# Graph layers: nine groups counted late and not stored, 22 groups multiplied in layer 0, seven sets of features in ten as parts

## The chip, the core and the metric

The kernel runs on one core of a Trainium2 chip. The metric is the device time of one execution in microseconds (us); lower is better. The core has five engines with a queue of instructions each: PE (TensorE, matmuls; PEld are its weight loads), DVE (VectorE), ACT (ScalarE), POOL (GpSimd) and SP (SyncE, which here only issues DMAs). They wait for each other through semaphores.

## The reference

Two graph layers over 6250 nodes and 100000 edges, edges sorted by target, width 128, float32:

```python
def _layer(h, edge_feats, src, dst, deg, iso, Wn, Ws, Wi, num_nodes):
    msg = (h[src] + edge_feats) @ Wn.T
    agg = segment_sum(msg, dst, num_nodes) / maximum(deg, 1.0)[:, None]
    self_msg = where(iso[:, None], h @ Wi.T, h @ Ws.T)
    x = agg + self_msg
    return where(x >= 0, x, RRELU_SLOPE * x)
h = _layer(x, edge_attr, src, dst, deg, iso, Wn0, Ws0, Wi0, N)
h = _layer(h, edge_attr, src, dst, deg, iso, Wn1, Ws1, Wi1, N)
out = layernorm(x + h)
```

The kernel sums the features of the edges at each target once (both layers need the same sums) and adds, in each layer, the sums of the rows h[src].

## The kernel before

**Windows and groups.** 128 edges are a chunk, 4 chunks a window (196 windows), 16 chunks a group (49 groups). A window is summed on PE by products with one-hot matrices of 40 columns (`window_chunk`, `sum_chunk`), and DVE adds the result to `sums` (`take_window`, L738).

**Two ways to the rows h[src].** A window is *gathered*: POOL issues four indirect DMAs (`gather`, L512) into one of five slots of `rows`, and PE multiplies three bf16 parts of each row (L1197, rows). Or a whole group is *counted and multiplied*: for each chunk DVE makes comparison matrices (`make_codes`: `is_lane` L725, `is_code` L727, `is_before` L721 once for four chunks, six chunks ahead), PE makes counts in two products plus a small one (`count_piece`, L1246 and L1250) in banks of `ps_count`, ACT casts them into one of three buffers of `counts` (`keep_chunk`, L1051), and PE multiplies the counts with all 49 tiles of the nodes in three parts, 147 products of 136 columns (`multiply`, L1258). DVE adds that with one instruction (`take_dense`, L760).

**Layer 0.** 31 groups (`KEPT`) are counted, each is stored to HBM (`store_counts`, L426, 1764 KB), and 20 of them (`USED`) are multiplied at once. The other 116 windows are gathered. The features of a window are float32; PE takes them as such (a product of two passes, the records "f32 x2") or, for 78 windows (`SPLIT_RATE` 0.4), as three bf16 products after DVE has cut them in two instructions (`split_feats`, L710 and L712).

**Layer 1.** All 31 groups' counts are loaded again in seven cuts each (`load_counts`, L448, 252 KB, ring of three buffers) and multiplied; 72 windows are gathered, from the rows that layer 0 made. The first gather of layer 1 waits until all of them are stored (`parts_stored`).

**Order.** Each engine's program is written in beats: one window a beat, 196 and some beats in layer 0, 72 and some in layer 1. `plan_layer0` says how many chunks are counted in a beat (`BUILDS`, 2 or 3 before) and how many tiles are multiplied (`MULTIPLIED`, 5 or 6 before). Nodes are worked on in trios of 384 (17 trios): each passes through stages (`STAGE`) spread over some beats: inputs, degrees, products, activate, parts, keep. In layer 1 `PIECES1` says how many cuts are multiplied by each beat, three or four a beat.

**Coupling.** PE begins window n only when DVE has added window n - 2 (two banks `ps_win`) and has made its one-hots (four ahead); a count piece waits until ACT has emptied the bank (three banks); POOL begins a gathered window when the window five gathers back has been summed. DVE's beat k adds window k - 1, then cuts the features of window k + 2, does node stages and makes codes.

## Time and profile before

| | us |
|---|---|
| median of 3 runs | 1080.71 (1080.55 to 1085.12) |
| the profiled execution's own time | 1087.57 |
| its span, first to last instruction | 1085.8 |
| window 0 begins | 40.0 |
| windows 12 to 191 (180 beats of layer 0) | 87.3 to 671.2 |
| last window of layer 0 summed | 686.4 |
| layer 1's gathers | 703.1 to 1068.1 |

The profile's busy time of PE counts overlapping records, and a matmul's recorded length has its latency in it; what a matmul costs in a stream is the distance from its start to the next start, read in a timeline. A wait says which engine's result ended an idle time. The time of a stretch goes to the engine whose work fills it or that the others wait for.

### The profile page before, as it was taken

How to read it: one execution, taken by the hardware profiler on the slowest of the kernel's cores; microseconds unless marked ns; L12 is line 12 of the kernel's file. 1: busy time of each engine (PE TensorE's matmuls, PEld its weight loads, DVE VectorE, ACT ScalarE, POOL GpSimd, SP SyncE). 2: the span in 40 equal slices, each digit the busy share in tenths (PEclk: the TensorE clock that was granted, in tenths of full speed). 3: DMA queues.
4: the chain of work that ended last, by engine and by line, in shares of the span. 5: the costliest groups of instructions: out<-in, count | busy, mean ns of one | idle time of the engine just before them, and what ended most of it. 6: DMA issues, size and time to landing. Idle time of an engine off the chain costs nothing.

```text
span 1085.8 us, 38527 instructions
## 1 busy us (share of the span) xinstructions
PE 933.4 (86%) x14592; PEld 869.7 (80%) x14592; DVE 691.7 (64%) x2388; ACT 513.5 (47%) x1143; POOL 760.0 (70%) x757
## 2 busy tenths in 40 slices
PE   1599989899998998998889987479999999999982
PEld 0488888788988887887878886479999999998981
DVE  7878987898897898887878885312243233423333
ACT  6478777777887777776767774100000000000000
POOL 8367757777767777767777657077777777777772
PEclk9999999999999999998989998599999999999995
DMA  9468877878887797797778778799988898888741
GB/s 303 154 198 269 298 250 261 268 258 277 278 287 260 241 325 249 225 314 243 230 231 282 250 253 298 225 367 316 281 260 271 252 280 273 262 265 276 225 117 52
DMA packets 154041, 277.50 MB, mean 256 GB/s; under 512 B 21458, under 2 KB 112572, under 8 KB 149884
## 3 DMA queue, kind: packets, MB, share of 16 engines
q1 hardware_dynamic: 93504, 184.10, 50.5%
q0 software_dynamic: 35584, 72.92, 22.9%
q10 hardware_dynamic: 24764, 17.95, 5.2%
q8 instruction: 120, 1.97, 0.7%
q14 instruction: 69, 0.57, 0.2%
HBM read 202.58 MB, written 72.30 MB: 253 GB/s over the span
## 4 chain that ended last, share of the span: by engine, by line
PE 48%; issue 6%; DVE 4%; DMA 3%; ACT 2%; POOL 2%; ACTq 1%; DVEq 0%; SPq 0%; POOLq 0%
PE ps_count L1258 25%; PE ps_win L1197 7%; PE ps_dense L1258 6%; PE ps_count L1246 5%; PE ps_self L1310 3%; PE ps_node L1323 2%; POOL rows L512 2%; DMA rows<-x_parts_rows,idx 1%; ACT counts L1051 1%; DVE is_code L727 1%; DMA counts<-counts_kept 1%; PE ps_win L1204 1%; DMA h_parts_rows<-row_parts 1%; DVE is_lane L725 1%; PE ps_self L1292 0%
## 5 line engine op out<-in xcount | busy, mean ns | idle before, releaser
L512 POOL DMA_INDIRECT rows<-x_parts_rows,idx x442 | 450.9, 1020 | 189.0 <-issue 127.9
L1051 ACT CAST counts<-ps_count 128x294 f32 x992 | 436.4, 504 | 151.2 <-PE ps_count L1246 69.1
L512 POOL DMA_INDIRECT rows<-h_parts_rows,idx x286 | 278.1, 972 | 111.9 <-issue 84.8
L1246 PE MATMUL ps_count<-is_code,is_lane 128*128 128x294 bf16 x992 | 301.9, 311 | 35.3 <-ACT counts L1051 33.4
L1258 PE MATMUL ps_dense<-counts,h_parts 128*128 128x136 bf16 x2940 | 311.0, 224 | 3.9 <-DVE sums L760 2.2
L1258 PE MATMUL ps_count<-counts,h_parts 128*128 128x136 bf16 x4557 | 282.1, 223 | 10.0 <-DMA counts<-counts_kept 10.0
L1258 PEld LDWEIGHTS ps_count<-counts,h_parts 128*128 128x128 bf16 x4557 | 273.5, 98 | 10.7 <-DMA counts<-counts_kept 10.4
L1197 PE MATMUL ps_win<-onehot,feats 128*128 128x40 f32 (+1 forms) x1564 | 245.0, 236 | 22.9 <-DVE sums L738 11.3
L1258 PEld LDWEIGHTS ps_dense<-counts,h_parts 128*128 128x128 bf16 x2940 | 210.2, 98 | 39.7 <-ACT counts L1051 5.1
L1197 PEld LDWEIGHTS ps_win<-onehot,feats 128*128 128x128 f32 (+1 forms) x1564 | 205.9, 158 | 28.1 <-issue 19.9
L727 DVE TENSOR_SCALAR is_code<-codes,code 128x637 bf16<-128x637 f16 x496 | 197.9, 399 | 0.0
L1197 PE MATMUL ps_win<-onehot,rows 128*128 128x40 bf16 (+1 forms) x2224 | 149.0, 186 | 32.4 <-issue 29.6
L738 DVE TENSOR_TENSOR sums<-sums,ps_win 128x80 f32 (+1 forms) x268 | 59.1, 220 | 184.0 <-PE ps_win L1197 134.1
L1063 ACT COPY self_sums<-ps_self 128x384 f32<-128x384 f32 (+1 forms) x34 | 16.1, 475 | 321.7 <-PE ps_self L1310 321.7
L1197 PEld LDWEIGHTS ps_win<-onehot,rows 128*128 128x128 bf16 (+1 forms) x2224 | 130.3, 112 | 36.5 <-issue 33.4
L725 DVE TENSOR_SCALAR is_lane<-column,lane 128x128 bf16<-128x128 bf16 x496 | 135.9, 274 | 36.7 <-PE ps_count L1250 34.7
L1246 PEld LDWEIGHTS ps_count<-is_code,is_lane 128*128 128x128 bf16 x992 | 108.3, 110 | 46.1 <-ACT counts L1051 40.5
L1250 PE MATMUL ps_count<-is_before,is_lane 128*128 128x49 bf16 x465 | 88.7, 191 | 0.0
L697 DVE TENSOR_TENSOR onehot<-column,rel 128x160 f32<-128x160 bf16 x268 | 84.8, 318 | 1.6 <-issue 1.6
L712 DVE TENSOR_TENSOR feats<-feats_rest 128x512 bf16<-128x512 f32 x78 | 58.4, 749 | 2.7
L710 DVE TENSOR_TENSOR feats_rest<-feats 128x512 f32<-128x512 f32 x78 | 53.2, 682 | 6.6 <-DMA feats<-in_edges_dram 6.5
L1197 PE MATMUL ps_win<-onehot,feats_rest 128*128 128x40 bf16 x310 | 56.0, 182 | 0.0
(99 smaller groups left out, 784.7 us busy)
## 6 DMA issues: line engine op xcount, KB each, us to landing
counts_kept<-counts SPq DMA_DIRECT2D x31, 1764.0 KB
counts<-counts_kept SPq DMA_DIRECT2D x217, 252.0 KB, 4.4
feats<-in_edges_dram SPq DMA_DIRECT2D x196, 256.0 KB
rows<-x_parts_rows,idx POOLq DMA_INDIRECT x442
x_parts_rows<-h_parts SPq DMA_DIRECT2D x7, 672.0 KB, 7.7
h_parts<-h_parts_rows SPq DMA_DIRECT2D x7, 672.0 KB, 9.6
h_parts_rows<-row_parts ACTq DMA_DIRECT2D x16, 288.0 KB
rows<-h_parts_rows,idx POOLq DMA_INDIRECT x286
```

The lines of the kernel that those rows point to most:

```text
L512: nc.gpsimd.indirect_dma_start(rows[:, SUB * slot + c, :], None, table[:, :], bass.IndirectOffsetOnAxis(ap=indices[:, c:c + 1], axis=0)).t ...
L697: nc.vector.tensor_tensor(onehot[:, h:h + SUB, :], column[:, 0:W].unsqueeze(1).to_broadcast([P, SUB, W]), rel[:, chunk:chunk + SUB].unsque ...
L710: nc.vector.tensor_tensor(rest, f, upper(f), ALU.subtract).then_inc(feats_rest_made, 1)
L712: nc.vector.tensor_tensor(lower(f), rest, upper(rest), ALU.subtract).then_inc(feats_split, 1)
L725: nc.vector.tensor_scalar(is_lane[:, n % (AHEAD + 1), :], column[:, :], lane[:, col:col + 1], None, ALU.is_equal)
L727: nc.vector.tensor_scalar(is_code[:, n % AHEAD, :], codes[:, :], code[:, col:col + 1], None, ALU.is_equal).then_inc(codes_ready, 1)
L738: return nc.vector.tensor_tensor(s, s, p, ALU.add)
L1051: nc.scalar.copy(counts[:, j % BUFFERS, :, at(offset + first, count)], ps_count[:, q % BANKS, 0:count * TILES].rearrange("p (r t) -> p t r ...
L1197: last = nc.tensor.matmul(ps[:, 0, SUM * w:(SUM + 1) * w], left, right, start=first and i == 0, stop=final and i == len(lefts) - 1)
L1246: last = nc.tensor.matmul(ps[:, 0:count * TILES], is_lane[:, n % (AHEAD + 1), :], is_code[:, n % AHEAD, first * TILES:(first + count) * TI ...
L1250: last = nc.tensor.matmul(ps[:, 0:TILES], is_lane[:, (n - 1) % (AHEAD + 1), :], is_before[:, (n // 4) % 3, n % 4, :], start=False, stop=True)
L1258: last = nc.tensor.matmul(bank, h_parts[:, t, k, :], counts[:, b, t, 0:WIDE], start=(t == 0 and k == 0), stop=(t == TILES - 1 and k == PAR ...
```

## The change

- 22 groups are multiplied in layer 0 (13 and 37 join), so 108 windows are gathered there. Only these 22 are counted as before and stored. The plan is 2 chunks (now and then 1) and 6 or 7 tiles a beat.
- The other 9 (`LATE`: 1, 4, 10, 16, 22, 25, 28, 34, 46) are counted last and not stored. The first two are counted in layer 0's last 16 beats into two of the three buffers; the other seven in layer 1 between the products (`BUILDS1`: 112 chunks in 39 of its beats 1 to 49, mostly three a beat, one count chunk before each cut), each into the buffer that the group two before left. DVE makes the codes and ACT the casts in layer 1 too. Count pieces then use two banks, and the products of groups alternate between `ps_dense` and the third bank of `ps_count`.
- Counts of the 22 are loaded into the third buffer alone, one ring of seven cuts: 154 loads, not 217. The first seven are issued at beat 191 of layer 0.
- In layer 1 the first beat holds 14 cuts (the first two groups), then exactly three a beat.
- `SPLIT_RATE` is 0.7: 136 windows have their features cut by DVE, 58 more.

Core of the diff:

```diff
+def plan_layer1(order, late, built, beats, first, per_chunk, most):
+    chunks = late * per_chunk
...
+    while pos < len(order) or built < chunks:
+        target = first + max(0, (len(order) - first) * k // beats)
+        while pos < min(target, len(order)):
+            p, last = order[pos]
+            if p is not None and ends.get(p, k) >= k:
+                break
+            if p is not None and last:
+                done[p] = k
+            pos += 1
+        upto.append(pos)
+        now = []
+        while len(now) < most and built < chunks:
+            p = built // per_chunk
+            if p >= 2 and done.get(p - 2, k) >= k:
+                break
...
-    USED = sorted([g for g in KEPT if g % 3 == 0] + [7, 19, 31, 43])
-    JOBS, BUILDS, MULTIPLIED, BUILT_BEAT, DONE_BEAT = plan_layer0(KEPT, USED, 188, BUFFERS, GC, TILES, 5.6, 8)
+    USED = sorted([g for g in KEPT if g % 3 == 0] + [7, 13, 19, 31, 37, 43])
+    LATE = [g for g in KEPT if g not in USED]
+    JOBS = USED + LATE
+    BUILDS, MULTIPLIED, BUILT_BEAT, DONE_BEAT = plan_layer0(len(USED), 176, BUFFERS, GC, TILES, 6.2, 8)
+    LATE_BUFFERS = [len(USED) % BUFFERS, (len(USED) + 1) % BUFFERS]
+    RING = (len(USED) + 2) % BUFFERS
...
-    SPLIT_RATE = 0.4
+    SPLIT_RATE = 0.7
...
+    PIECES = [(i, c) for i in range(2) for c in range(CUTS - 1)] + [(i, CUTS - 1) for i in range(2)]
+    PIECES += [(i, c) for i in range(2, len(KEPT)) for c in range(CUTS)]
...
+    COUNT_BANK = [q % BANKS if q < LATE_COUNTS else q % 2 for q in range(COUNTS)]
...
-            def load_counts(q):
+            def load_counts(l):
+                i, cut = PIECES[LOADED[l]]
...
+                if l >= CUTS:
+                    sp.wait_ge(cut_multiplied, LOADED[l - CUTS] + 1)
...
-                    for j in range(len(JOBS)):
+                    for j in range(len(USED)):
                         if BUILT_BEAT[j] == k - 1:
                             store_counts(j)
+                    if k == max(LAST_MULTIPLY + 2, WINDOWS - FEATS):
+                        for l in range(CUTS):
+                            load_counts(l)
...
             def layer1():
...
                     node_stage1(k)
+                    make_late_codes(k)
...
             def begin_job(j):
+                b = buffer_of(j)
+                if j >= len(USED) + 2:
+                    act.wait_ge(cut_multiplied, LAST_PIECE[KEPT.index(JOBS[j - 2])] + 1)
...
                 for k in range(BEATS[1]):
+                    keep_chunks(BUILDS1[k] if k < len(BUILDS1) else ())
...
+            def multiply_piece(s):
+                i, cut = PIECES[s]
+                j = JOBS.index(KEPT[i])
+                if s in LOAD_OF:
+                    pe.wait_ge(counts_loaded[cut], 16 * (LOAD_OF[s] // CUTS + 1))
+                elif cut == 0:
+                    pe.wait_ge(piece_kept, 2 * GC * (j + 1))
...
+                    while q < q1 or s < s1:
+                        if q < q1:
+                            count_piece(q)
+                            count_piece(q + 1)
+                            q += 2
+                        if s < s1:
+                            multiply_piece(s)
+                            s += 1
```

**What moves on PE in layer 0.** The second half of beat 100; the rows with `is_code` and `is_before` count, those with `h_parts` multiply. Before:

```order
L1246 MATMUL ps_count<-is_code,is_lane 128x343
L1250 MATMUL ps_count<-is_before,is_lane 128x49
L1258 MATMUL ps_dense<-counts,h_parts 128x136 x3
L1246 MATMUL ps_count<-is_code,is_lane 128x294
L1197 MATMUL ps_win<-onehot,feats 128x40
L1197 MATMUL ps_win<-onehot,rows 128x40 x3
L1246 MATMUL ps_count<-is_code,is_lane 128x343
L1250 MATMUL ps_count<-is_before,is_lane 128x49
L1258 MATMUL ps_dense<-counts,h_parts 128x136 x3
L1197 MATMUL ps_win<-onehot,feats 128x40
L1197 MATMUL ps_win<-onehot,rows 128x40 x3
L1204 MATMUL ps_win<-onehot,ones 128x40 x4
```

and now (the lines have moved by 83):

```order
L1329 MATMUL ps_count<-is_code,is_lane 128x343
L1333 MATMUL ps_count<-is_before,is_lane 128x49
L1341 MATMUL ps_dense<-counts,h_parts 128x136 x6
L1280 MATMUL ps_win<-onehot,feats 128x40
L1280 MATMUL ps_win<-onehot,feats_rest 128x40
L1280 MATMUL ps_win<-onehot,feats 128x40
L1280 MATMUL ps_win<-onehot,rows 128x40 x3
L1329 MATMUL ps_count<-is_code,is_lane 128x294
L1341 MATMUL ps_dense<-counts,h_parts 128x136 x3
L1280 MATMUL ps_win<-onehot,feats 128x40
L1280 MATMUL ps_win<-onehot,feats_rest 128x40
L1280 MATMUL ps_win<-onehot,feats 128x40
```

Each float32 product of features has become three bf16 products; this half of the beat holds two count products of 294 and 343 columns where it held three, and nine products with the counts where it held six. The beat counts 2 chunks instead of 3.

**What moves on PE at the start of layer 1.** Before:

```order
L1333 MATMUL ps_node<-ident,h_row 128x128 x2
L1258 MATMUL ps_count<-counts,h_parts 128x136 x63
L1197 MATMUL ps_win<-onehot,rows 128x40 x12
L1258 MATMUL ps_count<-counts,h_parts 128x136 x63
L1197 MATMUL ps_win<-onehot,rows 128x40 x12
```

and now:

```order
L1422 MATMUL ps_node<-ident,h_row 128x128 x2
L1341 MATMUL ps_dense<-counts,h_parts 128x136 x126
L1341 MATMUL ps_count<-counts,h_parts 128x136 x126
L1341 MATMUL ps_dense<-counts,h_parts 128x136 x21
L1341 MATMUL ps_count<-counts,h_parts 128x136 x21
L1280 MATMUL ps_win<-onehot,rows 128x40 x12
L1329 MATMUL ps_count<-is_code,is_lane 128x294
L1329 MATMUL ps_count<-is_code,is_lane 128x343
L1341 MATMUL ps_dense<-counts,h_parts 128x136 x21
L1329 MATMUL ps_count<-is_code,is_lane 128x294
L1329 MATMUL ps_count<-is_code,is_lane 128x343
L1333 MATMUL ps_count<-is_before,is_lane 128x49
```

Fourteen cuts stand ahead of the first window, and from the next beat each cut has a counted chunk ahead of it.

**What moves on SP at the end of layer 0.** Before:

```order
L426 DMA counts_kept<-counts 128x7056
L387 DMA feats<-in_edges_dram 128x512 x2
L414 DMA h_in<-in_x_cols_dram 128x256
L421 DMA x_trio<-in_x_rows_dram 128x2x128
L435 DMA h_parts<-h_parts_rows 128x7x384 x6
L448 DMA counts<-counts_kept 128x1008 x7
L435 DMA h_parts<-h_parts_rows 128x7x384
L384 DMA wts<-in_wn_dram 128x128
L384 DMA wts<-in_ws_dram 128x128
L384 DMA wts<-in_wi_dram 128x128
L448 DMA counts<-counts_kept 128x1008 x210
```

and now:

```order
L484 DMA x_trio<-in_x_rows_dram 128x3x128
L450 DMA feats<-in_edges_dram 128x512 x2
L512 DMA counts<-counts_kept 128x1008 x7
L477 DMA h_in<-in_x_cols_dram 128x256
L484 DMA x_trio<-in_x_rows_dram 128x2x128
L498 DMA h_parts<-h_parts_rows 128x7x384 x7
L447 DMA wts<-in_wn_dram 128x128
L447 DMA wts<-in_ws_dram 128x128
L447 DMA wts<-in_wi_dram 128x128
L512 DMA counts<-counts_kept 128x1008 x147
```

The last store of counts, which stood ahead of the last features, is gone, and seven loads of counts stand ahead of the last trio's inputs and of the node rows.

## Rows read from the trace of the kernel before

**Rows 1.** Busy time by stretch; columns: stretch, length, busy per engine, clock, DMA share, GB/s.

```profile
87.30:671.20 583.90, 531.46 (x8254) 482.46 (x8250) 488.51 (x1706) 439.13 (x1004) 421.52 (x413) 0.98 0.80 264
671.20:703.10 31.90, 16.31 (x137) 15.04 (x137) 11.41 (x34) 3.54 (x8) 5.39 (x6) 0.55 0.74 246
703.10:1068.10 365.00, 332.58 (x5697) 328.13 (x5697) 117.42 (x439) 12.63 (x32) 278.06 (x286) 0.98 0.84 261
```

**Rows 2.** Groups by line, PE, layer 0: count, busy us, mean ns, idle before.

```profile
L1246 PE MATMUL ps_count<-is_code,is_lane 128*128 128x343 bf16 x458 | 145.0, 317 | 33.6 <-ACT counts L1051 33.2
...
L1204 PE MATMUL ps_win<-onehot,ones 128*128 128x40 bf16 x720 | 46.7, 181 | 0.0
```

**Rows 3.** Waits of DVE, layer 0: us in total, times, longest.

```profile
DVE is_lane L725 <- PE ps_count L1250: 29.5, 46, 3.0
```

**Rows 4.** Timeline of PE in layer 0: start, us, operation.

```profile
216.72 0.36 PE L1197 MATMUL ps_win<-onehot,feats 128*128 128x40 f32 x2
216.91 0.24 PE L1197 MATMUL ps_win<-onehot,rows 128*128 128x40 bf16 x3
217.00 0.31 PE L1246 MATMUL ps_count<-is_code,is_lane 128*128 128x343 bf16 x1
...
217.17 0.34 PE L1258 MATMUL ps_dense<-counts,h_parts 128*128 128x136 bf16 x3
217.35 0.29 PE L1246 MATMUL ps_count<-is_code,is_lane 128*128 128x294 bf16 x1
217.47 0.31 PE L1197 MATMUL ps_win<-onehot,feats 128*128 128x40 f32 x2
...
219.05 0.18 PE L1197 MATMUL ps_win<-onehot,feats 128*128 128x40 bf16 x1
...
219.20 0.28 PE L1246 MATMUL ps_count<-is_code,is_lane 128*128 128x294 bf16 x1
```

**Rows 5.** Timeline of DVE in layer 0.

```profile
214.23 0.35 DVE L721 TENSOR_TENSOR is_before<-column,before 128x196 bf16<-128x196 bf16 x1
214.50 0.25 DVE L725 TENSOR_SCALAR is_lane<-column,lane 128x128 bf16<-128x128 bf16 x1
...
214.96 0.46 DVE L725 TENSOR_SCALAR is_lane<-column,lane 128x128 bf16<-128x128 bf16 x1
...
215.51 0.22 DVE L738 TENSOR_TENSOR sums<-sums,ps_win 128x80 f32 x1
...
215.88 0.68 DVE L710 TENSOR_TENSOR feats_rest<-feats 128x512 f32<-128x512 f32 x1
...
217.23 0.24 DVE L725 TENSOR_SCALAR is_lane<-column,lane 128x128 bf16<-128x128 bf16 x1
```

**Rows 6.** Groups by line, POOL, layer 0.

```profile
L512 POOL DMA_INDIRECT rows<-x_parts_rows,idx x413 | 422.2, 1022 | 162.7 <-issue 119.7 <-PE ps_win L1204 43.0
```

**Rows 7.** Groups by line, POOL, layer 1.

```profile
L512 POOL DMA_INDIRECT rows<-h_parts_rows,idx x286 | 278.1, 972 | 111.9 <-issue 84.8 <-DMA h_parts_rows<-row_parts 25.0 <-PE ps_win L1197 2.1
```

**Rows 8.** Timeline of DVE at the end of layer 0.

```profile
679.07 0.69 DVE L710 TENSOR_TENSOR feats_rest<-feats 128x512 f32<-128x512 f32 x1 [6.06 <-DMA feats<-in_edges_dram]
```

**Rows 9.** Timeline of POOL: the first gather of layer 1.

```profile
703.13 0.94 POOL L512 DMA_INDIRECT rows<-h_parts_rows,idx  x1 [25.02 <-DMA h_parts_rows<-row_parts]
```

**Rows 10.** Timeline of PE between the layers: the first product of layer 1.

```profile
705.44 5.36 PE L1258 MATMUL ps_count<-counts,h_parts 128*128 128x136 bf16 x63 [9.96 <-DMA counts<-counts_kept]
```

**Rows 11.** Timeline of PE in layer 1.

```profile
740.05 3.89 PE L1258 MATMUL ps_count<-counts,h_parts 128*128 128x136 bf16 x63
743.77 0.46 PE L1197 MATMUL ps_win<-onehot,rows 128*128 128x40 bf16 x12
744.08 0.91 PE L1323 MATMUL ps_node<-wts,sums 128*128 128x128 f32 x6
744.83 0.34 PE L1258 MATMUL ps_count<-counts,h_parts 128*128 128x136 bf16 x3
```

**Rows 12.** Line L448: loads of counts, issue to landing.

```profile
DMA to landing us min/median/max: 3.1/4.4/12.0
```

More of the change, by code:

```diff
@@ L3, with plan_layer0 @@
 from contextlib import ExitStack
-def plan_layer0(kept, used, beats, buffers, per_chunk, tiles, tiles_per_beat, head):
-    plain = [g for g in kept if g not in used]
-    jobs, first = [], list(used)
-    while first or plain:
-        for some, count in ((first, 2), (plain, 1)):
-            jobs += some[:count]
-            del some[:count]
-    total = len(jobs) * per_chunk
+def plan_layer0(jobs, beats, buffers, per_chunk, tiles, tiles_per_beat, head):
+    total = jobs * per_chunk
     builds, pieces, built = [], [], 0
     build_beat, done_beat = {}, {}
-    waiting = [j for j, g in enumerate(jobs) if g in used]
-    k, tile = 0, 0
-    while built < total or waiting:
+    k, job, tile = 0, 0, 0
+    while built < total or job < jobs:
         now = []
@@ L33, in plan_layer0 @@
         cut = None
-        if waiting and build_beat.get(waiting[0], k) < k:
-            j = waiting[0]
-            cut = (j, tile, min(tiles, tile + int((k + 1) * tiles_per_beat) - int(k * tiles_per_beat)))
+        if job < jobs and build_beat.get(job, k) < k:
+            cut = (job, tile, min(tiles, tile + int((k + 1) * tiles_per_beat) - int(k * tiles_per_beat)))
             tile = cut[2]
             if tile == tiles:
-                done_beat[j] = k
-                waiting.pop(0)
+                done_beat[job] = k
+                job += 1
                 tile = 0
@@ L43, in plan_layer0 @@
         k += 1
-    return jobs, builds, pieces, build_beat, done_beat
+    return builds, pieces, build_beat, done_beat
+def plan_layer1(order, late, built, beats, first, per_chunk, most):
+    chunks = late * per_chunk
+    ends, done, builds, upto, pos = {}, {}, [], [0], 0
+    for p in range(built // per_chunk):
+        ends[p] = -1
+    k = 0
+    while pos < len(order) or built < chunks:
[13 more added lines that the diff above has]
+                break
+            now.append(built)
+            built += 1
+            if built % per_chunk == 0:
+                ends[p] = k
+        builds.append(now)
+        k += 1
+    return upto, builds
 def gnn_resnorm_kernel(nc, x_rows, x_cols, src, dst, edges, wn0, ws0, wi0, wn1, ws1, wi1, out):
@@ L103, in gnn_resnorm_kernel @@
     LAST_MULTIPLY = max(DONE_BEAT.values())
+    late_chunk, k = len(USED) * GC, BUILT_BEAT[len(USED) - 1] + 1
+    while late_chunk < (len(USED) + 2) * GC:
+        late = late_chunk // GC
+        if k == len(BUILDS):
+            BUILDS.append([])
+        while len(BUILDS[k]) < 2 and late_chunk < (late + 1) * GC and DONE_BEAT[late - BUFFERS] < k:
+            BUILDS[k].append(late_chunk)
+            late_chunk += 1
+        k += 1
     ORDER0 = [(3 * u + i, j) for u in range(STEPS) for j in range(GW) for i in range(3)]
@@ L127, in gnn_resnorm_kernel @@
         beat = sum(g < 3 * u + 3 for g, j in ORDER1)
-        pieces = CUTS * sum(g < 3 * u + 3 for g in KEPT)
+        pieces = max([LAST_PIECE[i] + 1 for i, g in enumerate(KEPT) if g < 3 * u + 3])
         beat = max(beat, next(k for k, q in enumerate(PIECES1) if q >= pieces))
@@ L474, in _ @@
                 load_weights(1)
-                for q in range(CUTS, PIECES):
-                    load_counts(q)
+                for l in range(CUTS, len(LOADED)):
+                    load_counts(l)
             with sp.Else():
@@ L899, in layer0 @@
                 for k in range(BEATS[0]):
-                    for j in USED_JOBS:
+                    for j in range(len(USED)):
                         if DONE_BEAT[j] == k - 1:
@@ L928, in layer1 @@
                 node_stage1(0)
-                for k in range(1, BEATS[1]):
-                    while added < PIECES1[min(k, len(ORDER1))] // CUTS:
-                        dve.wait_ge(cut_multiplied, CUTS * (added + 1))
+                for k in range(BEATS[1]):
+                    if k == 0:
+                        make_late_codes(0)
+                        continue
+                    while added < len(KEPT) and LAST_PIECE[added] < PIECES1[min(k, len(ORDER1))]:
+                        dve.wait_ge(cut_multiplied, LAST_PIECE[added] + 1)
                         take_dense(KEPT[added], WINDOWS + min(k - 1, len(ORDER1)), len(USED) + added)
@@ L1050, in keep_chunk @@
                         act.wait_ge(piece_kept, q - 1)
-                    nc.scalar.copy(counts[:, j % BUFFERS, :, at(offset + first, count)],
-                                   ps_count[:, q % BANKS, 0:count * TILES].rearrange("p (r t) -> p t r", t=TILES)
+                    nc.scalar.copy(counts[:, buffer_of(j), :, at(offset + first, count)],
+                                   ps_count[:, COUNT_BANK[q], 0:count * TILES].rearrange("p (r t) -> p t r", t=TILES)
                                    ).then_inc(piece_kept, 1)
```

101 lines of the change are left out of this document (57 added, 44 removed).

## Prediction

> **How the profile was read.** First the busy time by stretch [rows 1]: 180 beats of layer 0 take 583.9 us, the gap to layer 1's first gather 31.9, layer 1's gathers 365.0, the tail 17.7. They have different limits.
>
> **Layer 0 before.** L1204 stands four times in each window, so its 720 records are 180 beats [rows 2], 3.244 us each. No engine is full: DVE is busy 488.5 of 583.9, ACT 439.1, POOL 421.5 [rows 1]. PE's 531.5 is too high a figure, since its records overlap, so I price its work from start to start [rows 4]: a tile's three products 0.18 us (217.17 to 217.35), a chunk's counts 0.17 + 0.12, with the longest gaps 0.31; a float32 chunk of features 0.19 and its rows 0.09 (216.72 to 217.00); the same chunk cut into parts, rows included, 0.15 (219.05 to 219.20). With 457 chunks, 935 tiles, 108 float32 and 72 cut windows and 15 trios (about 2.3 us each) PE has 516 us of work in 584. Of the 68 left, 33 stand in one wait: the second count piece for ACT to empty its bank [rows 2]. DVE in turn waits 29.5 us for PE's counting [rows 3], and ACT's casts wait for PE. So layer 0 is a chain of three engines, each 77 to 88% occupied, in lock step within a beat or two.
>
> POOL is close too. Its gathers in layer 0 are 1022 ns with 0.3 us between, 5.2 to 5.3 us a window, and it is blocked for 43 us because PE has not freed a slot [rows 6]; PE waits for rows hardly at all there. It isn't the limit before.
>
> **Layer 1 before.** POOL makes 286 gathers in 365.0 us [rows 1], 5.07 us a window; each takes 972 ns and almost all idle time is the 0.3 us between two of them, 84.8 in sum, with 2.1 us of waiting for PE [rows 7]. PE needs less: 63 products in 3.72 us (740.05 to 743.77), the window 0.31 and the node products 0.75 for one part of a trio [rows 11], some 2.1 for a whole trio every 4.2 beats, 0.5 a beat: 4.54 us against 5.07. So layer 1 lasts as long as its gathers, from the moment at which the last node rows are stored, 703.13 [rows 9].
>
> **The change, part 1: the 180 beats.** By the tables that plan the beats, beats 12 to 191 now hold 353 chunks (104 fewer, the two late groups included), 1035 tiles (100 more), 126 cut windows (54 more) and 96 gathered ones (8 fewer).
> - PE: -104 x 0.31 = -32; +100 x 0.18 = +18; a chunk cut into parts saves 0.28 - 0.15 = 0.13, for 54 windows of four -28; 8 windows' rows, -3. Sum -45: 471 us of work.
> - ACT: 208 casts fewer. It falls from 439 busy to about 335, and with two chunks a beat a cast has 0.7 us where it had 0.5, so the wait of 33 us on the bank should nearly go.
> - DVE: a chunk's two comparisons cost 0.46 (214.50 to 214.96) and a fourth of `is_before`, 0.27 / 4 (214.23 to 214.50): 0.53; the two cuts of a window's features cost 1.35 (215.88 to 217.23) [rows 5]. -104 x 0.53 = -55, +54 x 1.35 = +73, two more additions +1: +19. Before, the same prices for everything that DVE does there sum to 480; now 499.
>
> What was hidden decides: PE gets 45 us less, but DVE 19 us more, and DVE is now the fullest engine. Its floor is 499, a beat of 2.77. The beats are coupled within one or two, so a beat costs roughly the larger of its PE and DVE work. Laid out beat by beat at these prices, that larger value averages 3.26 before, where 3.244 was measured. Now: 15 beats hold a trio's products, some 4.6 us on PE; the other 165 have DVE at 2 x 0.53 + 0.37 (addition and one-hot, 215.51 to 215.88) + 1.35 = 2.8, or 1.06 + 0.37 and a node stage of about 1.1 to 1.3 instead of the cut, against 2.5 on PE, 2.87 as the mean of the larger. (69 + 474) / 180 = 3.02. 180 x 3.02 = 543: **-40 us**. Bounds: 2.88 a beat (DVE 96% occupied), -65; 3.15 (DVE 88%), -17.
>
> **Part 2: head and tail of layer 0.** The first 12 beats count 31 chunks instead of 39, 8 x 0.31: -2. At the end DVE waited 6.06 us for the last features [rows 8], issued right behind the last store of 1764 KB. That store is gone; seven loads of the same sum come behind the features. The last windows are all gathered, so POOL holds part of it: -3 (bounds -6 and +4, if the loads delay the last rows and trio's inputs).
>
> **Part 3: between the layers.** The chain from the last window to 703.13 is untouched. PE sat there, 16.3 of 31.9 us busy [rows 1], and waited 9.96 us for loaded counts [rows 10]. Now those are loaded earlier and 14 cuts stand in this place, 14 x 1.24 = 17 us of products, of which most fit before the first rows arrive. First gather unmoved: 0.
>
> **Part 4: layer 1.** PE does the other 203 cuts in 68 beats, and 112 chunks x 0.31 = 35 us of counting, in 39 beats: 3.72 + 0.31 + 0.5 + 0.93 = 5.46 in a counting beat, 0.39 over POOL's 5.07; 4.53 in the others, 0.54 under. The longest run is 16 counting beats, 6 us late, on top of some 2 to 5 before it. POOL is blocked only when PE is more than four windows, 20 us, behind. The 22 beats after beat 49 give back 12 us. So the counting is hidden by POOL's pace; without that cover it would cost 35. The new waits: the ring holds one group, seven cuts, so a load has about 11 us from the freeing of its place to its use, where landing took 4.4 (worst 12.0, in the burst at the start) [rows 12]; ACT's clearing of a buffer and late casts stand behind node work in its queue. DVE has 117 of 365 us busy [rows 1] and takes 112 x 0.53 = 59 more. I take +3, bounds 0 and +15. Stores and loads of 16 MB each fall away; in layer 1 no wait on the row of PE shows that they cost anything: 0.
>
> POOL's own pace might suffer from the codes beside it. Layer 0's gathers take 1022 ns with DVE at 84%, layer 1's 972 with DVE at 32% [rows 1, 6, 7]; 50 ns x 286 = 14 us if codes were the cause and stood beside all of them. Laid side by side in the trace, the long gathers of layer 0 stand beside the float32 cuts of features more often than the short ones do, and beside the codes equally often; cuts are made in layer 0 alone. So I take none of it. The Trainium skill speaks against me here: SBUF — State Buffer, Who interferes with whom, says that VectorE's scalar-comparison instructions in their two-port modes lock GpSimd out while it writes descriptors, and that the float32 two-tensor form does not. By that rule layer 1 would take up to 14 us more and layer 0 nothing; the rows' 50 ns do not tell which form causes them.
>
> **Sum.** -40 - 2 - 3 + 0 + 3 = -42. The profiled execution, 1087.6, becomes 1045.6; it lies 7 above the median of 1080.7, so the median becomes **1039**.
>
> **Rivals.**
> 1. *DVE takes the chain's place more than I allow* (15%): beats of 3.15, -17 there, sum -19: 1062. For: no engine was over 88% before, and cuts are long instructions ahead of codes. Against: DVE's waits before were for PE's counting.
> 2. *PE or the ring falls behind in layer 1* (12%): 0.07 us more per chunk, as ACT's wait costs in layer 0 (33 / 458), and late loads, make a counting beat 5.8; lateness passes 20 us once and 12 us stay: 1048 to 1051.
> 3. *Codes slow the gathers* (8%): +14 in layer 1: 1053.
> 4. *DVE runs nearly full* (8%): 2.88 a beat, -65 in place of -40: 1014.
> 5. *Slower than before* (4%). DVE keeps the share of time busy that it had, 83.7%, because its waits are part of each hand-over with PE and not slack: (488.5 + 19) / 0.837 = 606 for the 180 beats, +22; with +12 in layer 1, 1110. It decides from a share of 86% down, where the beats' saving is gone. Against: the gaps before are waits for count pieces, of which there are a fifth fewer.
>
> **Chances.** The forecast's own case, 1030 to 1048, has 53%; the rivals as given. A range of **1017 to 1066** reaches over rivals 1 to 3 and most of 4, and leaves out rival 5 and a few in 100 on each side. A measurement of this kernel tells 0.5% (5 us) from no change: faster by more than that 0.93, within it 0.03, slower 0.04.
>
> **What would show it.** Layer 0's 180 beats at 540 us, with DVE busy above 90% of it, no wait of PE for ACT over 10 us in sum, and DVE's waits for counting mostly gone; DVE's wait on the last features shorter; the first gather of layer 1 near 656; gathers of layer 1 in 365 to 370 us with POOL still not waiting for PE; PE's idle time there small and standing after beat 50. I am wrong if the beats are above 3.15 (DVE's waits then name whom it waits for), if POOL waits for PE in layer 1, or if its gathers there are near 1020 ns.

## The result, and the profile after

The changed kernel takes **1102.98 us** by the median of five runs (1095.04 to 1106.52), the kernel before 1080.86 beside it (1080.55 to 1085.12): a ratio of **1.0176**, 95% interval 1.0147 to 1.0204. Slower by 1.8%, where 1039 was forecast and the range ended at 1066. Two executions of the runs further down are left out of their ratios: one of e2_three took 4911.54 us and one of e1_rate04 1090.95.

The profiled execution of the changed kernel is the quickest of its five, 1095.04 with a span of 1093.3. Busy time by stretch, with the columns of [rows 1] (stretch, length, busy time and count of PE, PEld, DVE, ACT and POOL, granted clock, share of the DMA engines, GB/s): the same 180 beats, the gap to layer 1's first gather, and layer 1's gathers.

```profile
82.90:666.80 583.90, 511.58 (x8363) 462.52 (x8364) 497.42 (x1594) 363.67 (x789) 400.72 (x384) 0.94 0.73 236
666.80:695.30 28.50, 22.57 (x221) 21.60 (x222) 12.39 (x39) 3.75 (x9) 3.40 (x4) 0.64 0.76 243
695.30:1076.20 380.90, 362.08 (x5925) 348.99 (x5926) 174.39 (x663) 116.73 (x263) 279.51 (x286) 0.98 0.71 202
```

The 180 beats take 583.9 us, to the tenth what they took before, although ACT's busy time fell from 439 to 364. PE's busy time fell by 20 us (531 to 512), less than the 45 of the forecast, and its granted clock from 0.98 to 0.94. Window 12 begins 4.4 us sooner, the gap is 3.4 shorter, and layer 1's gathers take 15.9 us longer. So two terms are off: the -40 of layer 0 is missing, and layer 1 costs 16 in place of 3.

The waits of PE and DVE in the 180 beats (us in total, times, longest), to be read against [rows 2, 3]:

```profile
PE ps_win L1280 <- DVE sums L803: 32.4, 49, 2.5
PE ps_dense L1341 <- DVE sums L825: 13.6, 12, 2.4
PE ps_count L1329 <- ACT counts L1127: 12.7, 17, 2.5
...
DVE feats_rest L775 <- PE ps_win L1287: 35.8, 23, 4.3
DVE sums L803 <- issue: 26.0, 15, 4.2
...
DVE is_lane L790 <- PE ps_count L1333: 3.6, 4, 1.8
```

and of the kernel before, two rows that [rows 2, 3] leave out:

```profile
PE ps_win L1197 <- DVE sums L738: 11.3, 10, 2.7
...
DVE sums L738 <- issue: 28.2, 15, 4.0
```

What was to go went: PE's wait for ACT's casts fell from 33 to 12.7 us and DVE's for counting from 29.5 to 3.6. In their place stands a wait that the kernel before did not have: DVE, about to cut features, waits 35.8 us until PE has finished a window. PE in turn waits 46 us for additions, where it waited some 13 before. And one row has stayed: a gap before DVE's additions in which the profile shows nothing that it waits for ("issue"), 28.2 us before and 26.0 now, of which the prediction says nothing.

In layer 1 the largest waits of the three engines concerned (695.3 to 1076.2):

```profile
PE ps_count L1329 <- ACT counts L1127: 14.6, 11, 3.5
...
DVE rstd L921 <- ACT std L1167: 57.8, 12, 6.8
...
POOL rows L577 <- PE ps_win L1280: 20.3, 25, 5.3
```

POOL, which set the pace before and waited 2.1 us for PE [rows 7], now waits 20.3. Its gathers themselves are as long as before, 977 ns where 972 stood in [rows 7]:

```profile
L577 POOL DMA_INDIRECT rows<-h_parts_rows,idx x286 | 279.5, 977 | 125.6 <-issue 81.1 <-DMA h_parts_rows<-row_parts 24.2 <-PE ps_win L1280 20.3
```

### The profile page after: what moved, and what is told of

The parts are those of the page before. It is cut to its first block, busy times and chain, and to the rows that moved or that the text cites. A ratio compares the mean times of both kernels' runs of the same rounds, so it can differ in the third digit from the quotient of the medians.

```text
span 1093.3 us, 39483 instructions
## 1 busy us (share of the span) xinstructions
PE 946.5 (87%) x15022; PEld 874.7 (80%) x15022; DVE 761.0 (70%) x2506; ACT 536.5 (49%) x1143; POOL 738.7 (68%) x725
## 4 chain that ended last, share of the span: by engine, by line
PE 42%; DVE 7%; issue 3%; ACT 2%; DMA 2%; ACTq 1%; DVEq 0%; SPq 0%
PE ps_dense L1341 15%; PE ps_count L1341 11%; PE ps_count L1329 5%; PE ps_win L1280 4%; PE ps_self L1399 3%; PE ps_node L1412 2%; DVE is_code L792 1%; ACT counts L1127 1%; DMA h_parts<-h_parts_rows 1%; DVE feats_rest L775 1%; DVE is_lane L790 1%; DVE h_rest L926 1%; DMA h_parts_rows<-row_parts 1%; DVE onehot L762 0%; PE ps_self L1381 0%
## 5 line engine op out<-in xcount | busy, mean ns | idle before, releaser
L1127 ACT CAST counts<-ps_count 128x294 f32 x992 | 458.9, 502 | 320.3 <-PE ps_count L1329 170.9
L1341 PE MATMUL ps_dense<-counts,h_parts 128*128 128x136 bf16 x5586 | 466.4, 227 | 20.6 <-DVE sums L825 13.6
L1341 PEld LDWEIGHTS ps_dense<-counts,h_parts 128*128 128x128 bf16 x5586 | 371.5, 100 | 54.2 <-issue 12.4
L1280 PE MATMUL ps_win<-onehot,feats 128*128 128x40 bf16 (+1 forms) x1564 | 221.0, 214 | 42.1 <-DVE sums L803 33.0
L1280 PEld LDWEIGHTS ps_win<-onehot,feats 128*128 128x128 bf16 (+1 forms) x1564 | 178.8, 132 | 57.3 <-issue 47.3
L1341 PE MATMUL ps_count<-counts,h_parts 128*128 128x136 bf16 x2205 | 142.2, 223 | 0.0
L1341 PEld LDWEIGHTS ps_count<-counts,h_parts 128*128 128x128 bf16 x2205 | 131.6, 98 | 2.5
L775 DVE TENSOR_TENSOR feats_rest<-feats 128x512 f32<-128x512 f32 x136 | 93.2, 686 | 40.4 <-PE ps_win L1287 35.8
L777 DVE TENSOR_TENSOR feats<-feats_rest 128x512 bf16<-128x512 f32 x136 | 101.9, 749 | 4.7
L1280 PE MATMUL ps_win<-onehot,feats_rest 128*128 128x40 bf16 x542 | 99.1, 183 | 0.0
```

The costliest lines, as they stand in the source:

```text
L775: nc.vector.tensor_tensor(rest, f, upper(f), ALU.subtract).then_inc(feats_rest_made, 1)
L777: nc.vector.tensor_tensor(lower(f), rest, upper(rest), ALU.subtract).then_inc(feats_split, 1)
L1127: nc.scalar.copy(counts[:, buffer_of(j), :, at(offset + first, count)], ps_count[:, COUNT_BANK[q], 0:count * TILES].rearrange("p (r t) -> ...
L1280: last = nc.tensor.matmul(ps[:, 0, SUM * w:(SUM + 1) * w], left, right, start=first and i == 0, stop=final and i == len(lefts) - 1)
L1341: last = nc.tensor.matmul(bank, h_parts[:, t, k, :], counts[:, b, t, 0:WIDE], start=(t == 0 and k == 0), stop=(t == TILES - 1 and k == PAR ...
```

## Three suspects, and how they were told apart

**Two buffers for the remainder (layer 0).** `split_feats(k + 2)` writes the remainder of window k + 2 into one of two buffers of `feats_rest` and first waits for PE to have summed the window cut two cuts earlier, `SPLIT[i - 2]`. With four sets in ten that window lies three or more windows back and is done. With seven in ten it lies only two back in 65 of the 136 cuts, which is window k, the one that PE is working on in this beat. DVE then does its cut, node work and codes after PE's beat instead of beside it.

**The load of seven columns (layer 0).** Each window is added at a column that DVE's sequencer reads from a table, seven at once, right ahead of every seventh addition. The rival to both: that DVE's waits are simply part of each hand-over with PE (rival 5 of the prediction) and only move when one is taken away.

**ACT's order in layer 1.** In a beat with both node steps ACT first copies the self products of trio u + 1, which PE makes at the end of its beat, and then takes the root for trio u, for which DVE waits. That did not matter while ACT had nothing else to do there; now the next casts, and on DVE the next codes, stand behind it. Rivals: PE simply has too much work, the ring of one buffer loads late, or codes slow the gathers. The timelines of one such place, PE, then ACT, then DVE (start, us, operation, in brackets the idle time before it and what ended it):

```profile
891.37 1.40 PE L1341 MATMUL ps_dense<-counts,h_parts 128*128 128x136 bf16 x21
896.28 0.69 PE L1329 MATMUL ps_count<-is_code,is_lane 128*128 128x294 bf16 x2 [3.51 <-ACT counts L1127]
...
896.84 2.56 PE L1341 MATMUL ps_dense<-counts,h_parts 128*128 128x136 bf16 x21
```

```profile
891.30 0.48 ACT L1139 COPY self_sums<-ps_self 128x384 f32<-128x384 f32 x1 [17.09 <-PE ps_self L1399]
...
891.69 0.30 ACT L1167 ACTIVATE std<-mv,eps 128x3 f32<-128x3 f32 x1
...
893.67 0.68 ACT L1116 COPY counts<-zeros 128x588 f32<-128x588 f32 x1 [1.68 <-DVE h_rest L926]
895.55 0.89 ACT L1127 CAST counts<-ps_count 128x294 f32 x2 [1.20 <-issue]
```

```profile
892.02 0.18 DVE L921 RECIPROCAL rstd<-std 128x3 f32<-128x3 f32 x1 [5.47 <-ACT std L1167]
```

ACT waits for PE's self products until 891.30; DVE waits 5.47 us, until 892.02, for the root behind that copy; ACT waits 1.68 us for DVE's normalizing before it may store, clears a buffer, stands 1.20 us for which the profile names nothing, and makes the first cast at 895.55; PE stands 3.51 us for it. Behind the pause the same 21 products take 2.56 us instead of 1.40.

## Experiments, first round: each part undone or mended alone

All ratios are to the kernel before, run on the same chip beside them; the changed kernel's is 1.0176. The lengths of beats and gathers are those of the profiled executions.

**e1_rate04.** One part undone:

```diff
-    SPLIT_RATE = 0.7
+    SPLIT_RATE = 0.4
```

> The changed kernel with four sets of features in ten cut (as before) in place of seven; all else of the change stays. Theory A (the cutting of window k+2 waits until PE has finished window k, because there are only two buffers for the remainder and at seven in ten every third or second cut finds both taken; VectorE then stands behind PE): the wait of feats_rest on PE (35.8 us, 23 times, in the changed kernel) is gone, VectorE's work falls by 54 x 1.35 = 73, PE's rises by 28, ACT has 208 casts fewer than before: the 180 beats take 540 to 560 us in place of 583.9, the whole about 1065 to 1080. Rival B (VectorE's waits are part of every hand-over with PE, the busy share stays at 85%): VectorE's 497 falls to about 424, beats of 500 or, where PE's 499 of work rules, about 575: the whole 1095. Rival C (the half clock or the slower gathers of the changed layer 0 set its pace): unchanged, 1100.

Measured: 1080.73 us, ratio 0.9948 (0.9915 to 0.9981). The 180 beats take 572.6 us; DVE's wait for a free remainder buffer is gone, and DVE is busy 437 us (76%), so it did not keep its share of 85%: rival 5's rule is out. Layer 1 takes 380.7, unchanged. The beats stay above the 540 to 560 that theory A gave, and DVE's gap with nothing shown is 48.3 us here. With the rate left alone, moving the counting gives 11 us in the beats; what it gives without that gap is seen in the third round.

**e2_three.** The same seven in ten, but a third buffer; the 512 bytes still lacking come from laying the setup's `lanes` into it and packing `std`, `rstd` and `eps`:

```diff
-        feats_rest = sb("feats_rest", [P, 2 * SUB, D])
+        feats_rest = sb("feats_rest", [P, 3 * SUB, D])
...
-                if i >= 2:
-                    dve.wait_ge(window_summed, SPLIT[i - 2] + 1)
+                if i >= 3:
+                    dve.wait_ge(window_summed, SPLIT[i - 3] + 1)
```

> The changed kernel with three buffers for the remainder of the cut features in place of two (the wait is then on the window three cuts back, always over by then); room is made by laying a table that only the setup uses into the third buffer and three small tiles into one. Nothing else differs. Theory A: the 35.8 us of waiting of feats_rest on PE go, and with them most of PE's 32.4 and 13.6 us of waiting for VectorE's additions; the 180 beats fall from 583.9 to 545 to 560, the whole to 1065 to 1080 by the median. Rival B (share of VectorE, hand-overs): the waits move to the one-hot codes and the additions, beats stay at 580 or above, the whole at 1095 to 1105. Layer 1's gathers stay at about 381 us by both.

Measured: 1080.13 us, ratio 0.9949 (0.9927 to 0.9970), 2.3% below the changed kernel. Beats 569.3 us. The wait of 35.8 us is gone from DVE's list, whose largest rows now are:

```profile
DVE sums L804 <- issue: 36.7, 17, 6.1
DVE is_lane L791 <- PE ps_count L1334: 9.2, 19, 1.1
```

The two buffers are shown as a cause. But the beats stay 26 us above the forecast, PE still waits 37 us for additions (46 in the changed kernel) where theory A had most of it gone, and the gap in which DVE waits for nothing shown has grown from 26.0 to 36.7.

**e3_swap.** Only ACT's two node steps of layer 1 change places:

```diff
-                    if (1, "self", k) in STAGE:
-                        ...
                     if (1, "normalize", k) in STAGE:
                         ...
                         store_any(u)
+                    if (1, "self", k) in STAGE:
+                        ...
```

> The changed kernel with ACT's two node steps of layer 1 in the other order within a beat: root and store of trio u first, then the copy of the self products of trio u+1. Theory L (in layer 1 VectorE's normalizing waits for ACT's root, which stands behind a copy that waits for the end of PE's beat; the next beat's codes and casts are all late, PE stands 3.5 us and runs at half clock behind it): the 57.8 us of waiting of rstd on ACT go, PE's 14.6 us on ACT's casts mostly too, and layer 1's gathers take 365 to 370 us in place of 380.9; the whole 1087 to 1092 by the median. Rival M (it is PE's sum of work, 112 x 0.31 us more, or the ring of one buffer): the gathers stay at 378 to 382. Rival N (codes slow the gathers themselves): a gather stays at 977 ns where 972 was measured, so at most 1.5 us. Layer 0 unchanged by all.

Measured: 1088.42 us, ratio 1.0026 (0.9992 to 1.0060). Layer 1's gathers take 366.3 us in place of 380.9:

```profile
706.30:1072.60 366.30, 358.12 (x5931) 345.61 (x5929) 174.87 (x664) 116.60 (x263) 277.99 (x286) 1.00 0.73 211
```

```profile
PE ps_count L1329 <- ACT counts L1127: 4.6, 9, 0.9
...
DVE rstd L921 <- ACT std L1167: 19.5, 6, 4.2
...
POOL rows L577 <- PE ps_win L1280: 8.5, 23, 1.8
```

PE's work, the ring and the codes are all as in the changed kernel, so none of the three rivals is the cause; 14.6 of layer 1's 15.9 us came from the order of two steps in ACT's queue. The granted clock of the stretch rose from 0.98, which the kernel before had too, to 1.00. Layer 0, the same program as in the changed kernel, took 594.8 us here where that kernel's profiled execution took 583.9: so executions of it differ by some 10 us. Set against this run, the third buffer is worth 23 us (594.8 to 571.4 in the next), which is what the medians say as well (25).

**e4_both.** The edits of e2_three and e3_swap together.

> Both mends at once: three buffers for the remainder and ACT's two node steps of layer 1 swapped. If theories A and L hold and are independent, the savings add: 25 to 40 us in layer 0 and 11 to 16 in layer 1, the whole at 1050 to 1065, below the kernel before (1080.8). By rivals B and M it stays at 1095 or above.

Measured: 1064.84 us, ratio 0.9795 (0.9755 to 0.9835). Layer 1's gathers 366.3, beats 571.4. The two causes are independent. By the ratios they are worth 2.3% and 1.5% of the kernel before, 25 and 16 us.

## Second round: the gap with nothing to wait for

DVE's timeline at one such gap in e4_both:

```profile
93.36 0.38 DVE L793 TENSOR_SCALAR is_code<-codes,code 128x637 bf16<-128x637 f16 x1
97.34 0.24 DVE L804 TENSOR_TENSOR sums<-sums,ps_win 128x80 f32 x1 [3.60 <-issue]
```

and the loads that its sequencer (DVEq) makes in the whole of e4_both, by count, with minimum, median and maximum in ns:

```profile
L797 DVEq TENSOR_LOAD <-base_i x71: 303/316/946, 86.2 to 1043.4; - x71
L797 DVEq TENSOR_LOAD <-base_o x28: 1037/1646/6094, 45.5 to 650.2; - x28
```

`base_o` is the table for layer 0, read seven columns at a time. The load in this gap begins at 93.1, while the engine is still at work, and takes 4.04 us, so it ends some 0.2 us before the addition starts. Over the 180 beats the loads of 1.04 us leave the engine idle for at most 0.2 us each, those of 1.6 to 2.0 for 0.2 to 1.3, and the ten of over 3 for 1.8 to 5.8. Loads of one or four columns (`base_i`) take 0.3 to 0.4 but for a few (the longest 0.95). In e4_both the engine's idle time behind loads sums to 42 us over the 180 beats, and in the kernel before to 45. Busy time does not count it, nor did the prediction. The experiments load one column in each beat, ahead of work that is long enough to hide it.

**e5_one_column.** On e4_both:

```diff
-                        if (k - 1) % 7 == 0:
-                            cols = load_columns(base_o, k - 1, 7)
-                        take_window(0, k - 1, cols[(k - 1) % 7], added)
+                        take_window(0, k - 1, cols[0], added)
                         if k - 1 + HOT < WINDOWS:
                             make_onehot(k - 1 + HOT)
+                    if k < WINDOWS:
+                        cols = load_columns(base_o, k, 1)
```

> e4_both (three buffers, ACT's steps swapped), and VectorE's sequencer loads the column of one window in each beat of layer 0, behind the addition and ahead of the cut, instead of seven columns at once every seventh beat right ahead of the addition. In e4_both the loads of seven take 1.63 us, nine of them 3.3 to 6.1, and 24 of the 48 gaps that stand behind such a load sum to 42 us in which VectorE does nothing. Theory C (these loads stand on the path: VectorE is the fullest engine, and PE waits 26.8 us for its additions): VectorE's additions wait under 10 us for nothing shown, PE's wait on them falls under 12, and the 180 beats go from 571.4 to 535 to 550, near the 543 that the prediction had: the whole at 1030 to 1045. Rival D (the gaps only take the place of waits for PE's counting): beats at 565 or above, whole 1058 to 1066. Rival E (what makes the long ones long comes with every load, also with one column): gaps of 2 to 4 us at other places, beats 560 to 600.

Measured: **1038.80 us**, ratio 0.9573 (0.9545 to 0.9602), 24 us below e4_both by the ratios.

```profile
82.60:632.90 550.30, 499.29 (x8366) 457.21 (x8363) 501.43 (x1593) 363.16 (x788) 403.80 (x383) 0.95 0.77 250
```

```profile
PE ps_count L1330 <- ACT counts L1128: 17.9, 22, 2.7
...
PE ps_win L1281 <- DVE sums L804: 8.1, 21, 0.7
```

```profile
L797 DVEq TENSOR_LOAD <-base_o x196: 298/307/1669, 43.6 to 644.3; - x196
```

196 loads of 0.31 us at the median take more of the sequencer's time than 28 did, but the longest is 1.7 us and nearly all are covered. DVE is busy 501 of 550 us (91%), PE's wait for additions fell from 26.8 us to 8.1. Theory C holds, rivals D and E do not. Beats are 550.3 us here and 543.9 in the repetition below; 543 was forecast.

**e6_seven_early.** On e4_both, seven columns again, at the same place as in e5_one_column:

```diff
-                        if (k - 1) % 7 == 0:
-                            cols = load_columns(base_o, k - 1, 7)
...
+                    if k < WINDOWS and k % 7 == 0:
+                        cols = load_columns(base_o, k, 7)
```

> e4_both with the load of seven columns kept at seven, moved one beat ahead, to the same place as in e5_one_column (behind the addition, ahead of cut, node steps and codes). Theory C: the sequencer has the addition and the one-hot, 0.37 us, in the engine's queue ahead of it, so a load of 1.63 us still empties the engine: it saves little of the 42 us, but no addition stands directly behind it, so PE waits less for additions; beats 558 to 570, whole 1052 to 1064. If the count of registers is what costs, this run stays near e4_both and e5_one_column does not; if the place alone matters, both are alike.

Measured: 1060.41 us, ratio 0.9782 (0.9744 to 0.9819), within its interval of e4_both. Beats 562.6. The gap has moved to what now stands behind the load:

```profile
DVE feats_rest L776 <- issue: 23.1, 10, 4.8
```

So the place is worth little, and the size of the load is what costs. Why a load of seven takes five times as long as one of four, and why some take up to 6.7 us (e2_three), no run here tells. The Trainium skill (Runtime: NRT & Kernel Launch, Instruction fetch mechanics) gives some 200 ns a register for loads that it describes as coming from HBM, where this table lies in SBUF. An estimate from that figure is 1.4 us for seven, near the median of 1.64 here, but 0.8 for four, where no load of layer 1 took more than 0.63 in the changed kernel. Here it does not go by a price per register, and the measured rows decide.

**e7_before_one_column.** The same edit on the kernel before.

> The kernel before with one column loaded in each beat, as in e5_one_column; nothing else. Theory C with its price in the kernel before: 45 us of gaps behind loads in the 180 beats, of which those that stand ahead of a late addition count; PE waits only 11.3 us for additions there, so 10 to 25 us: the whole at 1058 to 1073. If it is 1080 or above, the gaps were cover there (VectorE waits 29.5 us for counting), and only the changed kernel, in which VectorE is the fullest engine, feels them.

Measured: 1073.67 us, ratio 0.9914 (0.9880 to 0.9947), beats 570.6. Worth 9 us there and 24 to 32 in the changed kernel (e5_one_column, e9_after_one_column). DVE's waits for counting grew from 29.5 to 38.6 us when the gaps went, which fits that the gaps had partly stood where it would have waited anyway.

**e8_before_rate07.** The kernel before with `SPLIT_RATE = 0.7` and nothing else.

> The kernel before with seven sets of features in ten cut in place of four, with its two buffers; nothing else of the change. By the prediction's prices PE loses 28 us of work and VectorE gains 73: 561, above the 511 of before, so beats of 3.3 or more: 595 to 615, the whole 1092 to 1112. Theory A adds the wait of feats_rest on PE, 20 to 40 us of it, partly beside the waits for counting: 600 to 625, the whole 1097 to 1122. If it is at 1081 or below, cutting is free and the prediction's price for VectorE is wrong.

Measured: 1119.07 us, ratio 1.0333 (1.0298 to 1.0368). Beats 622.7, 38.8 more than before.

```profile
86.10:708.70 622.60, 524.91 (x8465) 464.10 (x8465) 552.37 (x1819) 435.45 (x1002) 432.26 (x417) 0.96 0.77 252
```

```profile
DVE feats_rest L710 <- PE ps_win L1204: 22.1, 18, 2.4
```

DVE's work rose by 64 us, where 73 was the price, and the wait for a buffer appears here too. As the kernels stand, with two buffers and loads of seven, cutting more sets is the part of the change that loses; the moving of the counting is the part that gains.

## Third round: independence, and the best rate

**e9_after_one_column.** The edit of e5_one_column on the changed kernel, two buffers and ACT's order left.

> The changed kernel with one column loaded per beat and nothing else: two buffers for the remainder and ACT's order as in the change. If the three causes are independent, layer 0's beats fall by the 21 us that e5_one_column took off e4_both, and layer 1's gathers stay at 381: the whole about 1075 to 1085. Theory A says that VectorE's wait on PE for a buffer stays in full (35 to 42 us), since it comes from the two buffers; if freeing the loads also removes that wait, the two are one cause and the whole is below 1070.

Measured: 1073.56 us, ratio 0.9883 (0.9833 to 0.9933), beats 562.4. The wait for a buffer is still there in full, and layer 1 takes 381.6:

```profile
DVE feats_rest L775 <- PE ps_win L1287: 38.1, 24, 2.9
```

Three causes, then, each of which shows without the others. They do not add up quite: mended singly they are worth 2.3, 1.5 and 2.9% of the kernel before, together (e5_one_column) 6.0%.

**e10_rate05, e11_rate04, e12_mended.** e5_one_column with `SPLIT_RATE` 0.5, with 0.4, and unchanged once more beside them.

> e5_one_column with five sets of features in ten cut in place of seven. By the prices: VectorE 36 x 1.35 = 49 us less (501 to 452), PE 36 x 4 x 0.13 = 19 more (460 to 479 of work). If VectorE alone bounds the beats they fall from 550.3 to below 520, the whole to 1010; if the larger of the two in each beat does, to 530 to 540, the whole 1020 to 1030; if PE with its waits for ACT does, they stay at 545 to 555.

> e5_one_column with four sets in ten cut, as in the kernel before. VectorE 54 x 1.35 = 73 us less than in e5_one_column (428), PE 28 more (488, by the float32 products). PE is then the fuller engine: beats 540 to 555, the whole 1030 to 1045. e1_rate04 had 572.6 with the loads of seven columns in place; the difference to it is the price of those loads when VectorE has room, 10 to 30 us if it is still paid.

> e5_one_column once more, beside the two rates and with five rounds: all three mends on the changed kernel. 1036 to 1043 as before, a ratio to the kernel before of 0.955 to 0.962; the yardstick for e10_rate05 and e11_rate04, which run on the same chip.

| cut in ten | median us | ratio (interval) | beats | DVE busy | PE waits for additions into `sums` | DVE waits for counting (two largest rows) |
|---|---|---|---|---|---|---|
| 7 (e12) | 1039.96 | 0.9587 (0.9545 to 0.9628) | 543.9 | 501.0 | 17.4 | 17.5 |
| 5 (e10) | **1025.28** | 0.9441 (0.9394 to 0.9488) | 529.1 | 459.3 | 4.9 | 33.6 |
| 4 (e11) | 1038.55 | 0.9578 (0.9531 to 0.9626) | 538.1 | 440.0 | 2.9 | 59.3 |

```profile
82.40:626.30 543.90, 493.28 (x8366) 452.10 (x8364) 501.00 (x1593) 363.01 (x788) 404.07 (x383) 0.97 0.78 253
```

```profile
84.80:613.90 529.10, 500.44 (x8223) 464.27 (x8220) 459.26 (x1521) 365.20 (x788) 393.30 (x383) 0.98 0.80 260
```

At seven in ten PE waits for DVE, at four DVE for PE; at five both work side by side longest. e10_rate05 is 5.6% faster than the kernel before and 7% faster than the changed one. e11_rate04 against e1_rate04 (538.1 and 572.6; at this rate no cut finds both buffers taken, and the order of ACT in layer 1 does not touch these beats) puts the loads of seven at 34 us, no less than where DVE is full: their gaps stand right ahead of additions, for which PE waited 17.8 us in e1_rate04. And with one column a beat and four sets in ten on both sides, moving the counting takes the beats from 570.6 (e7_before_one_column) to 538.1, 32 us, where with the loads of seven it gave 11. The larger part of what the change had to give was hidden behind them. With the mends, the step from four to seven sets in ten costs 6 to 12 us of beats (538.1 against 543.9 and 550.3).

## Why the prediction was wrong

**Part 1, the beats: -40 forecast; 0 measured, in an execution 8 us below the median of its kernel.** DVE's work was priced right: put at 499 us, it is 497.4. ACT's, put at 335, is 364 (a cast fewer saved 0.36 us, not 0.5), and still PE's wait for ACT and DVE's for counting went as said. The step that failed is "a beat costs roughly the larger of its PE and DVE work". It took PE and DVE to overlap freely within a beat or two and looked at no buffer that ties one to the other. With 54 more cuts over the same two buffers, half of the cuts are bound to PE's current window; 23 of them waited, and in those beats the costs add. The wait could have been found in the code from the spacing of the cuts; in the trace of before it never occurs, and so no row of it warned. Price: 25 us by the ratios.

**The same part, PE's work: -45 forecast, -20 measured.** The same work of PE in the 180 beats has busy times of 520.0, 511.6, 502.9, 499.3 and 493.3 us at granted clocks of 0.93, 0.94, 0.95, 0.95 and 0.97 (e3_swap, the changed kernel, e4_both, e5_one_column, e12_mended). The last is 38 below the kernel before, which had 0.98, so the price was nearly right and the clock took some of it back. No run separates the clock from the waits: the prices of the causes above hold both. The printed terms for PE's work before sum to 509, not 516, and ACT is 75% occupied, not 77; the -40 rests on neither.

**The same part, the calibration.** The rule gave 3.26 us a beat before, where 3.244 was measured, and that agreement was taken as proof. It was luck: the kernel before held some 45 us of idle time behind column loads, which the sum did not have, and with them gone (e7_before_one_column) it takes 3.17 a beat. With work only, the floor for DVE was 499; with the gaps it is, by an estimate from the 26 to 42 us of them, 525 to 541. e5_one_column and e12_mended, without gaps and without the buffer wait, take 550.3 and 543.9: near the rule's 543 once both are gone, with a rule that was a little high in the kernel before.

**Part 2** went the right way: -2 and -3 forecast, -4.4 and -3.4 measured, and DVE's wait of 6.06 us for the last features is gone. **Part 3** was forecast at 0: the stretch from window 192 to the first gather, which holds the end of part 2 and part 3, shrank by those 3.4 us in all.

**Part 4, layer 1: +3 forecast, +15.9 measured.** PE's work was as forecast: with ACT's order mended the gathers take 366.3, +1.3. The failed step is one that the prediction names and does not price: "ACT's clearing of a buffer and late casts stand behind node work in its queue". What stands there is a wait in a circle, ACT for the end of PE's beat, DVE for ACT, ACT for DVE, and only then the casts on which PE waits with two banks. Price: 14.6 us.

**Rivals.** Rival 1 had its sign and not its size. Two of the prediction's own signs of being wrong came: beats above 3.15, and POOL waiting for PE in layer 1. Rival 2 came nearest in layer 1, 9 to 12 us, by the wrong way. Rival 3 fell: with codes beside layer 1's gathers a gather takes 977 ns, and 966 to 981 in all runs, where 972 stood before and 1022 was asked. The Trainium skill (SBUF — State Buffer, Who interferes with whom) would have VectorE's comparisons lock GpSimd out where they run in a two-port mode. No row tells the mode; in layer 1 the measured 5 ns on a gather are at most 1.5 us in all, so by these rows it does not count here. Layer 0's gathers do lengthen with the cuts, as the prediction read the trace: 1015, 1030 and 1059 ns at four, five and seven sets in ten, with nothing else changed (e11_rate04, e10_rate05, e12_mended). In e12_mended those that stand beside a cut for over half a microsecond take 1137 on average, those that meet none 999. Rival 5 gave 1110, and 1103 came; its premise, that DVE keeps its busy share because waits are part of each hand-over, is refuted: the share went from 85% to 92% once two particular causes were removed. With 4% for it, and nothing for a new wait in layer 0, the range of 1017 to 1066 was too narrow for a change that rewrites who waits for whom.

## What to carry to other kernels

When more of the work passes through a buffer, count for each use how many steps back its last user lies: a wait that never occurs in the trace of before can become the largest of the trace after. Add to an engine's busy time the idle time that its sequencer causes ("issue") before you call the rest slack, and don't take a model that reproduces the old time as proof while such a row is unaccounted for. When work is put into a queue that had none, read what that queue waits for at each place, in order, even where the engine is idle most of the time.

## What of the hardware was not expected

- A load of seven table entries by VectorE's sequencer takes 1.64 us at the median and up to 6.7 (e2_three), one of a single entry 0.31 at the median and up to 1.9 (e9_after_one_column), none of layer 1's, of up to four, over 0.63 in the changed kernel. Long ones go with the program: of the 28 loads, counted from 0, numbers 2, 9, 10, 16, 22 and 23 take over 3 us in the changed kernel and in each of e1 to e4, and numbers 5, 6, 13, 19, 20, 22 and 26 in the kernel before and in e8_before_rate07. Why, no run tells. The loads of seven cost 24 us by e4_both and e5_one_column.
- After a pause of 3.51 us PE's next products ran at half speed, 2.56 us for 21 where 1.40 is usual; the granted clock of the stretch behind it is 0.60, of those around it 1.00. For most of that stretch TensorE thus ran at the lower of its two levels, 1.2 of 2.4 GHz. Busy time by stretch of the changed kernel:

```profile
889.00:894.00 5.00, 3.77 (x57) 3.50 (x53) 1.72 (x8) 1.02 (x3) 3.78 (x5) 1.00 0.51 145
894.00:902.50 8.50, 6.22 (x61) 5.75 (x62) 1.93 (x7) 2.79 (x7) 3.23 (x4) 0.60 0.53 144
902.50:911.00 8.50, 8.50 (x141) 8.11 (x138) 4.97 (x18) 3.90 (x10) 6.05 (x6) 1.00 0.67 179
```

  So the pause costs at least 5.8 us in place of 3.5: 1.16 and 1.14 more for the two pieces behind it.
